# First cross attention, first pass: four squares a head on GpSimd in place of three, two of them folded once, summed by VectorE in two halves, and ScalarE's loop written out

## The reference

```python
qk = jnp.einsum('bhqd,bhkd->bhqk', Q, K)          # 16 heads, 256 queries, 4096 keys, 16 wide
scores = qk / math.sqrt(dk)
mean_sim = scores.mean(axis=(-2, -1))
max_sim = scores.max(axis=-1).mean(axis=-1)
probs = jax.nn.softmax(scores, axis=-1)
entropy_proxy = jnp.var(probs, axis=-1, ddof=1).mean(axis=-1)
feats = jnp.stack([mean_sim, max_sim, entropy_proxy], axis=-1)
# two small layers turn feats into a temperature t for each head
attn = jax.nn.softmax(qk / (2.0 * t), axis=-1)
```

## Time and profile before

| what | us |
|---|---|
| median of 3 runs | 1378.09 |
| lowest and highest | 1377.07, 1380.81 |
| profiled execution, its own time | 1383.17 |
| its span | 1381.4 |
| first pass in it, about | 54 to 304 |

### The profile page before, as it was taken

The page is one execution under the profiler, slowest core; times in us unless marked ns, Lnnn a source line. Parts: engine busy times, 40 slices in busy tenths (PEclk is TensorE's granted clock), DMA queues, the critical chain, the costliest instruction groups (busy, mean ns, idle before and its releaser), DMA issues. The chain is left out here.

```text
span 1381.4 us, 25688 instructions
## 1 busy us (share of the span) xinstructions
PE 1127.1 (82%) x8423; PEld 692.4 (50%) x8423; DVE 823.8 (60%) x1510; ACT 893.1 (65%) x1206; POOL 630.4 (46%) x293
## 2 busy tenths in 40 slices
PE   7687877757999858989977778888888888858798
PEld 3343444433444436678862444544444444434687
DVE  6688888871110176562235787888878887945312
ACT  3599999976989724533322787888888888624110
POOL 2177778760000005000002888899999999900000
PEclk9799999987999968899995899999999999977899
DMA  7875545537555062014467888999989989534130
GB/s 251 241 225 124 130 108 134 126 92 152 112 110 107 0 197 75 1 49 153 152 220 244 322 311 303 303 325 328 325 313 326 319 319 337 192 98 141 46 137 8
DMA packets 97048, 257.51 MB, mean 186 GB/s; under 512 B 11193, under 2 KB 41305, under 8 KB 85466
## 3 DMA queue, kind: packets, MB, share of 16 engines
q1 hardware_dynamic: 96992, 256.79, 59.5%
HBM read 165.31 MB, written 91.92 MB: 186 GB/s over the span
## 5 line engine op out<-in xcount | busy, mean ns | idle before, releaser
L1934 POOL TENSOR_TENSOR xb_row<-xb_row,w_mask 128x1024 f32<-128x1024 f32 x128 | 419.1, 3286 | 241.0 <-DVE xb_row L1964 239.4
L1964 DVE TENSOR_TENSOR xb_row<-xb_cont_ps,xb_row 128x1024 f32<-128x1024 f32 x128 | 156.7, 1224 | 86.9 <-PE xb_cont_ps L1757 67.4
L1757 PE MATMUL xb_rel_ps<-xb_kk,xb_qq 32*128 32x512 f32 x496 | 147.9, 674 | 35.7 <-ACT xb_out L1882 33.8
L554 DVE TENSOR_REDUCE xa_stats<-xa_b_ps 128x1 f32<-128x1024 f32 x128 | 155.8, 1220 | 33.4 <-PE xa_b_ps L470 32.7
L1975 DVE CUSTOM_DVE_ANT_0 xb_row<-xb_row,xb_minus 128x1024 f32<-128x1024 f32 x128 | 171.8, 1342 | 0.0
L1887 ACT ACTIVATE xb_row<-xb_row,xb_ntop 128x2048 f32<-128x2048 f32 x64 | 128.3, 2005 | 56.4 <-DVE xb_ntop L1981 56.4
L1757 PE MATMUL xb_cont_ps<-xb_kk,xb_qq 32*128 32x512 f32 x528 | 157.9, 676 | 2.8 <-DVE xb_row L1964 1.7
L864 ACT ACTIVATE xa_probs<-xa_psT,xa_t_now 128x1024 f32<-128x1024 f32 x128 | 141.1, 1114 | 20.3 <-PE xa_psT L823 20.1
L1882 ACT COPY xb_out<-xb_rel_ps 128x1024 f32<-128x1024 f32 x124 | 124.8, 1006 | 40.5 <-PE xb_rel_ps L1757 25.2
L522 ACT ACTIVATE xa_exps<-xa_b_ps,xa_stats 128x1024 f32<-128x1024 f32 x128 | 141.3, 1108 | 14.0 <-DVE xa_stats L554 14.0
L1801 PEld LDWEIGHTS xb_turn_ps<-_ident,xb_row 128*128 128x128 f32 x1008 | 115.9, 148 | 55.1 <-issue 55.1
(11 more groups left out here) (367 smaller groups left out, 1832.7 us busy)
## 6 DMA issues: line engine op xcount, KB each, us to landing
xb_row<-rel_scores SPq DMA_DIRECT2D x128, 512.0 KB, 6.6
rel_scores<-xb_out SPq DMA_DIRECT2D x32, 1024.5 KB, 6.0
rel_scores<-xb_out SPq DMA_DIRECT2D x32, 1024.0 KB, 5.9
b_e_w<-in_L_ffn_e_w SPq DMA_DIRECT2D x32, 513.0 KB, 3.5
w_w<-in_L_ffn_w SPq DMA_DIRECT2D x24, 512.0 KB, 4.8
xa_k<-first_parts SPq DMA_DIRECT2D x24, 384.0 KB, 5.0
value_rows<-xa_values SPq DMA_DIRECT2D x16, 544.0 KB, 6.1
xb_kk<-key_blocks SPq DMA_DIRECT2D x17, 512.0 KB, 8.1
```

The costliest lines, as they stand in the source:

```text
L554: nc.vector.tensor_reduce(stats[:, c % 2, 0, u:u + 1], ps[:, slot % 4], AX, ALU.min).then_inc(s["min_ready"], 1)
L1757: mm = nc.tensor.matmul(out[:, k * BANK:(k + 1) * BANK], qq[rows, b, kind, t * P:(t + 1) * P], kk[rows, b, half], start=True, stop=True)
L1934: nc.gpsimd.tensor_tensor(row[:, held(c), at:at + SUB], row[:, held(c), at:at + SUB], mask[:, t, half * HALF + at:half * HALF + at + SUB], ...
L1964: nc.vector.tensor_tensor(row[:, held(c), at:at + SUB], cont_ps[:], row[:, held(c), at:at + SUB], ALU.add).then_inc(s["cont_out"], 1)
```

## The change

GpSimd squares quarters 1, 3, 5 and 7, and ScalarE 0, 2, 4 and 6. GpSimd folds its first two squares of a head twice, as before, and the last two once. The folded columns of the first two go to a buffer of 2 x 256 columns, those of the last two to one of 2 x 512, and neither is double buffered: the first fold of the first and third square waits for `unfolded`. VectorE's `unfold` has two halves: the first stands at the end of the same head, the second where `unfold` stood. ScalarE's loop over `it` becomes Python's, so that its 16 heads are written out.

```diff
--- before.py
+++ after.py
@@ -373,10 +373,12 @@
             squares = f.sb(inner, "squares", [P, QUARTER])
             stats = f.sb(inner, "stats", [P, 2, 3, NU])
             values = f.sb(inner, "values", [P, 2, H // 2, CPH, DV])
-            ACT_SQUARES, POOL_SQUARES = (0, 2, 3, 5, 6), (1, 4, 7)
-            NA, NG_SQ = len(ACT_SQUARES), len(POOL_SQUARES)
-            FOLDS, FOLDED = 2, QUARTER // 4
-            folded = f.sb(inner, "folded", [P, 2, NG_SQ, FOLDED])
+            ACT_SQUARES, POOL_SQUARES = (0, 2, 4, 6), (1, 3, 5, 7)
+            NA = len(ACT_SQUARES)
+            FOLDS = (2, 2, 1, 1)
+            POOL_STEPS = sum(n + 1 for n in FOLDS)
+            pool_begun = lambda h, n: POOL_STEPS * (h + 1) + sum(k + 1 for k in FOLDS[:n])
+            folded = [f.sb(inner, f"folded{n}", [P, 2, QUARTER >> folds]) for n, folds in enumerate((2, 1))]
             s = {n: f.sem("b_" + n) for n in ("scored", "projected", "product_out", "min_ready", "exp_done", "act_squared",
                                               "pool_product", "pool_folded", "unfolded", "kept", "ones_set", "edges_stored")}
             keys_stored = [f.sem(f"b_keys_stored{b}") for b in range(2)]
@@ -515,7 +517,7 @@
 
                     before, used = (h, u - 4) if u >= 4 else (h - 1, u + 4)
                     if used in POOL_SQUARES:
-                        act.wait_ge(s["pool_product"], (FOLDS + 1) * (NG_SQ * (before + 1) + POOL_SQUARES.index(used)) + 1)
+                        act.wait_ge(s["pool_product"], pool_begun(before, POOL_SQUARES.index(used)) + 1)
                     else:
                         act.wait_ge(s["act_squared"], NA * (before + 1) + ACT_SQUARES.index(used) + 1)
                     act.nop()
@@ -532,7 +534,7 @@
                     nc.scalar.activation(squares[:], exps[:, u % 4], ACT.Square,
                                          accum_out=stats[:, c % 2, 2, u:u + 1]).then_inc(s["act_squared"], 1)
 
-                with act.Fori(0, NB) as it:
+                for it in range(NB):
                     for c in range(HPB):
                         act.wait_ge(s["kept"], HPB * it + c + 1)
                         for j in range(NU // 2):
@@ -547,6 +549,7 @@
                 nc.vector.memset(values[:, :, :, :, DK:DV], 1.0).then_inc(s["ones_set"], 1)
                 dve.sem_inc(s["product_out"], NU // 2)
                 dve.sem_inc(s["kept"], 2)
+                dve.sem_inc(s["unfolded"], 2)
 
                 def minimum(it, c, u):
                     h, slot = HPB * it + c, u + u // 2
@@ -574,17 +577,17 @@
                         nc.vector.tensor_copy(dst, src.rearrange("p (k h d) -> p h k d", k=half, h=H // 2)
                                               ).then_inc(s["product_out"], 1)
 
-                def unfold(it, c):
+                def unfold(it, c, half):
                     h = HPB * it + c
-                    dve.wait_ge(s["pool_folded"], NG_SQ * (h + 1))
-                    nc.vector.tensor_reduce(stats[:, c % 2, 2, 1:NU:3], folded[:, c % 2], AX, ALU.add
+                    dve.wait_ge(s["pool_folded"], len(FOLDS) * h + 2 * half + 2)
+                    nc.vector.tensor_reduce(stats[:, c % 2, 2, 4 * half + 1:4 * half + 4:2], folded[half][:], AX, ALU.add
                                             ).then_inc(s["unfolded"], 1)
 
                 def keep(it, c):
                     h = HPB * it + c
 
                     dve.wait_ge(s["act_squared"], NA * (h + 2))
-                    dve.wait_ge(s["unfolded"], h + 1)
+                    dve.wait_ge(s["unfolded"], 2 * h + 4)
                     dve.wait_ge(s["exp_done"], NU * (h + 2))
                     nc.vector.tensor_reduce(stats_all[:, bass.ds(h, 1)].rearrange("p h k u -> p (h k u)"),
                                             stats[:, c % 2].rearrange("p k u -> p (k u)").unsqueeze(2), AX, ALU.add
@@ -603,40 +606,41 @@
                                 product_out(it - 1, HPB - 1, NU // 2 - 1)
                             minimum(it, c, 2 * j + 1)
                             if j == 1 and c > 0:
-                                unfold(it, c - 1)
+                                unfold(it, c - 1, 1)
                                 keep(it, c - 1)
                             elif j == 1 and not first:
-                                unfold(it - 1, HPB - 1)
+                                unfold(it - 1, HPB - 1, 1)
                                 keep(it - 1, HPB - 1)
+                            elif j == NU // 2 - 1:
+                                unfold(it, c, 0)
 
                 bodies(dve, body)
                 product_out(NB - 1, HPB - 1, NU // 2 - 1)
-                unfold(NB - 1, HPB - 1)
+                unfold(NB - 1, HPB - 1, 1)
                 keep(NB - 1, HPB - 1)
                 dve.wait_ge(s["kept"], H + 2)
 
             @block.gpsimd
             def _(pool):
-                pool.sem_inc(s["pool_product"], (FOLDS + 1) * NG_SQ)
+                pool.sem_inc(s["pool_product"], POOL_STEPS)
 
                 def square(it, c, u):
                     h, n = HPB * it + c, POOL_SQUARES.index(u)
-                    done = (FOLDS + 1) * (NG_SQ * (h + 1) + n)
+                    done = pool_begun(h, n)
                     pool.wait_ge(s["exp_done"], NU * (h + 1) + u + 1)
                     pool.wait_ge(s["pool_product"], done)
-                    if n == 0:
-                        pool.wait_ge(s["kept"], h + 1)
                     nc.gpsimd.tensor_tensor(rest[:], exps[:, u % 4], exps[:, u % 4], ALU.mult).then_inc(s["pool_product"], 1)
+                    if n % 2 == 0:
+                        pool.wait_ge(s["unfolded"], 2 * h + n // 2 + 1)
                     width = QUARTER
-                    for k in range(FOLDS):
+                    for k in range(FOLDS[n]):
                         width //= 2
                         pool.wait_ge(s["pool_product"], done + k + 1)
-                        out = rest[:, 0:width] if k < FOLDS - 1 else folded[:, c % 2, n]
-                        ins = nc.gpsimd.tensor_tensor(out, rest[:, 0:width], rest[:, width:2 * width], ALU.add)
-                        ins.then_inc(s["pool_product"], 1)
-                        if k == FOLDS - 1:
-                            pool.wait_ge(s["pool_product"], done + k + 2)
-                            pool.sem_inc(s["pool_folded"], 1)
+                        out = rest[:, 0:width] if k < FOLDS[n] - 1 else folded[n // 2][:, n % 2]
+                        nc.gpsimd.tensor_tensor(out, rest[:, 0:width], rest[:, width:2 * width], ALU.add
+                                                ).then_inc(s["pool_product"], 1)
+                    pool.wait_ge(s["pool_product"], done + FOLDS[n] + 1)
+                    pool.sem_inc(s["pool_folded"], 1)
 
                 with pool.Fori(0, NB) as it:
                     for c in range(HPB):
```

## The result

| | median us | lowest to highest | runs |
|---|---|---|---|
| before | 1377.58 | 1372.27 to 1380.81 | 4 |
| after | 1390.69 | 1388.06 to 1392.79 | 4 |

The median is 13.1 us longer, 0.95% of that of before. The ratio on record, which is not the quotient of these two medians, is 1.0107, with a 95% interval of 1.0084 to 1.0131. So the change makes the kernel about 1% slower. The forecast was +10.9 us, 1389 us. The two profiled executions differ by 4.9 us only (1388.06 and 1383.17), because that of before lies 5.6 us over its median and that of after 2.6 us under its own. So the pass itself is compared, from its first exponential to the end of its last `keep`: 249.3 us before, 261.2 after, **+12.0 us**.

What follows compares the result with a forecast made beforehand. ScalarE was taken to bound the pass at 15.02 us a head, then GpSimd at 15.7. 15 x (15.7 - 15.02) + 1.2 - 0.5 = +10.9 us on the 1378.09 median gave 1389 us, range 1380 to 1399.

Steps and rivals of the forecast that it cites:

- What bounds the kernel now: First pass over the 16 heads: ScalarE sets the pace, at an average of 15.02 us a head.
- The route: Exponential u+4 may not overwrite its slot before GpSimd's square of u; half the exponentials wait, some 2.5 us a head.
- GpSimd's work: Four squares, four folds to 512 columns and two to 256 take GpSimd 14.11 us a head.
- The handoffs: Semaphore waits between GpSimd's ten instructions a head: 0.32 + 0.30 + 1.00 us, making the head 15.7.
- The cover for its first half's sum: VectorE's new sum chain takes 5.4 us against GpSimd's 7.0 of work: 1.6 us of cover, no cost.
- Start and end: Pass's ends: first head unchanged, turns of GpSimd's loop add 1.2 us, the end gives -0.5.
- The range: Whole kernel's time: from 1380, the floor of the handoffs, to 1399 us.
- The rival that VectorE sets the pace, and faster: In the pass, GpSimd's cycle fits under VectorE's 14.67 us a head, saving 5.8 us: 1372; chance 0.09.
- Handoffs at their floor: GpSimd's handoffs at their least, 15.2 us a head: +2.6 us, 1381, no change that can be told; chance 0.14.
- TensorE at its lower clock in each head: TensorE slows after longer pauses in every head, cycle near 16.6 us: +24, 1402; chance 0.05.
- The rule against the change: Moving work to GpSimd costs time there; the skill's figure gives 2.2 us a square, about 20 us more.
- What would show it: Signs in the pass: GpSimd about 90% busy, ScalarE waiting for its squares some 2.5 us a head, one table load.

Runs made afterwards that it cites:

- e1: Kernel before with only ScalarE's loop over the 16 heads written out; 1368.27 us, 0.9947 of before.
- e8: Changed kernel with every square folded once and VectorE waiting for the fold's own count, no separate wait and increment; 1371.14 us, 0.9972 of before.
- e9: e8 with VectorE summing only 256 of the 512 columns of a head's first two squares; 1370.71 us, 0.9969 of before.
- e12: e8 with a head's fourth product copied out of PSUM by ScalarE instead of VectorE; 1371.68 us, 0.9965 of before.
- e5: Changed kernel with VectorE's first sum of a head moved later and the folded columns double buffered; 1388.29 us, 1.0105 of before.
- e4: Changed kernel without GpSimd's separate wait and increment after each last fold; VectorE waits for the fold's own count; 1375.40 us, 1.0001 of before.
- e3: Changed kernel with all four squares folded once, VectorE summing 512 columns of each; 1369.87 us, 0.9952 of before.
- e7: e4 with a second buffer for GpSimd's squares, so a square need not wait for the fold before it; 1369.83 us, 0.9972 of before.
- e10: e9 with each product summed over half of its depth, so work is left out; 1364.16 us, 0.9914 of before.

## Why the prediction was right

- **What bounds the kernel now.** That ScalarE set the pace before is shown for the turns of its loop: e1, which changes ScalarE alone, moves the time. For the heads of 14.5 us it is not shown: e8, e9 and e12 have a square less on ScalarE a head and GpSimd under 14, and stay at 14.5. So of the "up to 20 us" that the forecast gave to ScalarE's part alone, the square's 1.09 a head was worth nothing by itself; another chain, through the four PSUM buffers as far as argued above, stands at the same length.
- **The route.** The forecast had the exponentials wait for GpSimd's squares, through the slots of `exps`. This step was wrong, though the sum does not use it: no exponential came closer than 0.95 us to the end of the square in its slot. VectorE's sums wait for GpSimd (25.1 us from 54 to 310 us) and pass the delay on.
- **GpSimd's work.** Forecast 14.11 us a head, measured 14.15. Two folds took 1.285, not 1.267.
- **The handoffs.** This term was the least certain, and it is where the sum was mis-sized. Ahead of a square 0.25 was taken and 0.31 to 0.34 measured, 1.27 a head in place of 1.00. For the two first folds with a wait on `unfolded` 0.15 was taken and 0.08 measured, 0.16 in place of 0.30. The head became 15.90, not 15.7 (the forecast's own terms add up to 15.73). The trace had 0.43 us as a bound and the sequencer's rows 0.15; the value lay in the middle, not near the sequencer's rows.
- **VectorE.** The reduce over 512 columns took 685 ns (667 forecast). The cover for its first half's sum was claimed to suffice; VectorE did wait 18.8 us there in 16 waits, with ScalarE behind it. The forecast had named this as a sign of being wrong; e5 shows that no time hung on it.
- **Start and end.** The turns of GpSimd's loop cost 0.38 us each, as forecast (0.4). The end gave back 0.5, as forecast. The start was wrong: head 0's last square came at 71.56, 2.0 us earlier than the 73.57 that was taken for both, and 16.95 us after the first exponential in place of 18.56. In the second profile of the changed kernel it is 17.75.
- **The sum.** From last square of head 0 to that of head 15: 239.50 against 225.37, +14.1. The end -0.5, the start -1.6: +12.0, where the forecast had +10.9. From square to square the forecast had +11.4, so it was 2.7 short: 2.0 from the handoffs over 15 heads, 0.6 from the durations and 0.4 from rounding 15.73 down make 3.0, of which other roundings and the turns take 0.3. The start that it left out took back 1.6, or 0.8 in the second profile. So the closeness to 1.1 us is in part luck.
- **The range.** Its lower end, 1380, is the floor of the handoffs, 1381 by its sum. In that sum the turns of GpSimd's loop count 0.4 us, in the others 1.2; with 1.2 it is 1381.5. The upper end, 1399, comes from no sum: the upper bound of 16.6 us a head gives 1402.
- **The rival that VectorE sets the pace, and faster.** Refuted by e5 and by GpSimd's waits, which are its own. **Handoffs at their floor**: e4 is close to it (14.97 a head) and came out at 1.0001, but the change as it stands has the separate semaphore step. **TensorE at its lower clock in each head**: the granted clock was 0.95 from 54 to 300 us, but the heads without a turn of GpSimd's loop, 15.86 to 15.94, equal GpSimd's own sum, whether the clock over them was 0.89 or 1.00.
- **The rule against the change.** The square stayed at 1.89 us after the change (1894 ns over 63 of them). The estimate of 2.2 us, worked out from the 2.6 cycles an element of the Trainium skill (GPSIMD Engine Reference, Performance versus the Vector engine), had the direction right and the size too large.
- **What would show it.** GpSimd's busy share is 87% from 54 to 300 us, the stretch of the forecast's 75%, and 89% from 90 to 290 us (90% forecast). ScalarE is idle 2.5 us a head (2.5 forecast), and there is one table load. ScalarE's wait is put down to VectorE's minima, not to GpSimd's squares.

The forecast gave the three table loads 3.8 us if ScalarE's part stood alone. What it did not see is that the written-out loop alone is worth twice that, -0.5%, so that the change holds two parts of opposite sign, and that the loop is worth nothing once GpSimd is the bound.

## What to carry to other kernels

Before giving an engine more work, add up its work of one period with a handoff for every instruction, and compare with the average period, loop turns included; here that gave the head to 0.2 us, while busy shares gave nothing. (That the whole time came within 2 us is in part luck, as the start shows.) Look then at what stands between two dependent instructions: a separate wait and increment cost 0.24 us here, on the bound engine four times a head, and waiting for the instruction's own count gave all of it back. Cutting a bound engine's work pays only down to the next limit: here 14.5 us a head, which neither less work for VectorE (e9) nor a copy moved to ScalarE (e12) lowered. Time a change's parts apart: the part that won was hidden by the one that lost, and the simplest faster kernel (e1, 0.9947; e3 at 0.9952 cannot be told from it) has one line changed.

## What was not expected of the hardware

- Two dependent GpSimd instructions stand 0.08 us apart when the second waits by itself, 0.31 when a separate wait and an increment stand between, with the next square's register instruction and wait behind them (after against e4), and overlap by 0.04 when they are independent (e7).
- A table load of 1283 ns in a loop's body cost 7.6 us over three turns where ScalarE set the pace: more than the 3.8 us of the loads, since the head behind two of the turns was longer as well, both with a product at about half its speed (3.63 and 3.59 us, against 1.98 at the first turn, where the clock stayed at 1.00 and the next head was no longer).
- Making TensorE's work shorter lowered its granted clock, 1.00 to 0.90 from 90 to 290 us (e9 to e10), and some heads became longer than with the full work.
